# A post-norm decoder layer on one core: self attention by 32-row score strips with block turns on VectorE, and a new order around it

## What is computed

```python
# self attention: 16 heads of 64, no mask
q, k, v = split(x @ w_qkv)                     # (8, 16, 112, 64) each
attn = softmax(q @ k.T * 64 ** -0.5)
x = layernorm(x + (attn @ v) @ w_out + b_out)
# cross attention: 16 heads of 16, 375 keys, one mask for all
q, k, v = x @ Wq.T + bq, ctx @ Wk.T + bk, ctx @ Wv.T + bv
probs = softmax(where(mask == 0, -1e10, q @ k.T * 16 ** -0.5))
x = layernorm(x + (probs @ v) @ Wo.T + bo)
# one of 8 experts by argmax of x @ router.T, and a shared expert
y = down[e] @ (silu(gate[e] @ x) * (up[e] @ x))
x = layernorm(x + y + shared(x))
```

## Time and profile before

| | us |
|---|---|
| median of 3 runs | 432.59 (432.57 to 433.21) |
| profiled execution, its own time | 433.12 |
| its span, first to last instruction | 431.4 |
| TensorE busy | 408.3 (95%) |
| VectorE busy | 243.8 (57%) |
| ScalarE busy | 194.4 (45%) |
| GpSimd busy | 51.0 (12%) |

### The profile page before, as it was taken

The page is one execution under the profiler, slowest core; times in us unless marked ns, Lnnn a source line. Parts: engine busy times, 40 slices in busy tenths (PEclk is TensorE's granted clock), DMA queues, the critical chain, the costliest instruction groups (busy, mean ns, idle before and its releaser), DMA issues.

```text
span 431.4 us, 8970 instructions
## 1 busy us (share of the span) xinstructions
PE 408.3 (95%) x3130; PEld 287.5 (67%) x3131; DVE 243.8 (57%) x724; ACT 194.4 (45%) x580; POOL 51.0 (12%) x78
## 2 busy tenths in 40 slices
PE   8999999999999988999999999999988999999992
PEld 7767869778796855666666676666655475666661
DVE  1275765747566565666675767666764642244443
ACT  1164462433526446677567666766683101111220
POOL 4010010100101001000010101010100054212222
PEclk9999999999999999999999999999999999999998
DMA  8999000000000014040404050920000012112210
GB/s 249 364 378 274 12 0 2 0 2 2 1 2 0 2 37 147 2 183 2 185 2 183 7 179 4 366 108 2 2 2 2 1 62 98 57 56 68 70 40 28
DMA packets 15241, 34.25 MB, mean 79 GB/s; under 512 B 2381, under 2 KB 9150, under 8 KB 13920
## 3 DMA queue, kind: packets, MB, share of 16 engines
q1 hardware_dynamic: 13952, 30.72, 20.6%
q0 software_dynamic: 1104, 2.76, 1.8%
q10 hardware_dynamic: 144, 0.23, 0.2%
HBM read 27.27 MB, written 6.70 MB: 79 GB/s over the span
## 4 chain that ended last, share of the span: by engine, by line
PE 86%; DVE 5%; ACT 4%; issue 3%; POOL 0%; POOLq 0%; DVEq 0%; ACTq 0%
PE bank L437 11%; PE bank L638 9%; PE bank L451 7%; PE bank L619 6%; PE bank L507 6%; PE bank L815 6%; PE bank L536 5%; PE bank L655 4%; PE bank L905 4%; PE bank L881 4%; PE bank L887 4%; PE bank L529 4%; PE bank L468 3%; PE bank L494 3%; PE bank L827 3%
## 5 line engine op out<-in xcount | busy, mean ns | idle before, releaser
L1264 DVE CUSTOM_DVE_ANT_0 p<-bank,mask 112x375 f32<-112x375 f32 x128 | 62.7, 545 | 36.9 <-PE bank L619 36.9
L1023 ACT ACTIVATE p<-p,nm 112x375 f32<-112x375 f32 x128 | 74.4, 604 | 2.1 <-DVE nm L1264 2.0
L1030 ACT ACTIVATE pT<-bank 128x336 f32<-128x336 f32 x96 | 42.3, 441 | 44.4 <-PE bank L638 44.4
L638 PEld LDWEIGHTS bank<-ident,p 112*128 112x128 f32 (+1 forms) x384 | 38.1, 140 | 28.4 <-issue 23.1
L638 PE MATMUL bank<-ident,p 112*128 112x112 f32 (+1 forms) x384 | 53.8, 267 | 2.2 <-DVE nm L1264 2.0
L437 PE MATMUL bank<-x2T,arena 128*128 128x224 f32 x256 | 52.9, 354 | 0.0
L966 ACT ACTIVATE p<-bank,nm 112x112 f32<-112x112 f32 x128 | 43.5, 365 | 18.4 <-DVE nm L1134 18.3
L437 PEld LDWEIGHTS bank<-x2T,arena 128*128 128x128 f32 x256 | 46.8, 191 | 0.2
L352 POOL TENSOR_TENSOR rstd<-veps,minus_half 128x1 f32<-128x1 f32 x14 | 7.7, 549 | 289.8 <-DVE veps L1160 289.8
L1134 DVE TENSOR_REDUCE nm<-bank 112x4 f32<-112x448 f32 x32 | 19.2, 620 | 24.1 <-PE bank L468 24.1
L619 PE MATMUL bank<-kT,qz 32*112 32x375 f32 x256 | 28.8, 517 | 4.0 <-ACT x2T L992 2.5
(11 more groups left out here) (144 smaller groups left out, 595.1 us busy)
## 6 DMA issues: line engine op xcount, KB each, us to landing
arena<-in_ug SPq DMA_DIRECT2D x8, 1024.0 KB, 5.8
arena<-in_dn SPq DMA_DIRECT2D x8, 512.0 KB, 6.9
mid<-in_ctxT SPq DMA_DIRECT2D x8, 375.0 KB, 3.1
slots_s<-blank SPq DMA_DIRECT2D x14, 128.5 KB, 3.8
arena<-in_wqk SPq DMA_DIRECT2D x7, 256.0 KB, 5.6
slots_x<-blank SPq DMA_DIRECT2D x14, 128.0 KB, 6.7
p<-slots_s SPq DMA_DIRECT2D x9, 128.5 KB, 2.1
kT<-slots_x SPq DMA_DIRECT2D x9, 128.0 KB, 2.2
```

Source lines behind the costliest of these rows:

```text
L638: mm = pe.transpose(PE_T2[r][0:k1 - k0, t * S:(t + 1) * S], p2_rows[:, i % RING, k0:k1], ident[0:S, 0:S])
L1023: act.activation(p2[i % RING], p2[i % RING], ACT.Exp, bias=nm2[:, i % H:i % H + 1], scale=-1.0).then_inc(exp2, 1)
L1030: act.activation(pT2[:, i % RING], PE_T2[r][:, 0:KT * S].rearrange("p (k n) -> p k n", k=KT), ACT.Copy).then_inc(pt2_act, 1)
L1264: v.tensor_tensor_reduce(p2[i % RING], PE_S2[r][0:S, 0:S2], bias[:], 1.0, 3e38, ALU.add, ALU.min, accum_out=nm2[:, i % H:i % H + 1]).then_ ...
```

## The change

- *Scores.* The 112 query rows are cut into 4 blocks of 32 (`SQ`, `QB`); in odd batches the last has 16 rows. A score matmul now has 32 query columns, so eight run side by side: 2 row halves (head parity) x 4 column strips (four heads). A bank holds, for each of four heads on its strip of 32 partitions, 4 blocks of rows by 112 keys.
- *Softmax* works on all 128 partitions; its tiles are laid out by strip.
- *Turns.* TensorE's turns and VectorE's copies go; VectorE turns 32x32 blocks from `p1` to `pT1` in SBUF (`turn_blocks`). `p1` is padded to 128 columns, zeroed once by GpSimd.
- *Values.* `value1` sums over four blocks of 32 keys; eight matmuls side by side: 4 row strips (heads) x 2 column halves (parity), into four banks, one for each strip. The two `evac_o` each wait for both pairs.
- *Value projection.* `project_v1` writes the values by strip: 32 token columns x 4 strips x 256 columns. The weights' columns are reordered on the host (`by_strip`).
- *Order of a batch.* `out1` moves behind the second score group and into half of bank 7; the query scale's matmul goes to bank `PE_J1[0]`, and `project_v1(3, 0)` waits for the scale. Values stand before the last two projections of the batch.
- *Cross attention.* `project_k(0, b + 1)` moves ahead of the turns 2 and 3 of slot g = 0. The norm is split: the sum at the start of slot 0, moments at its end. `evac_x2` goes from ScalarE to the end of slot 1 on VectorE. In the last slots `out2(5)`, `turn_x2(5)`, the first router products and shared-expert products are reordered.

```diff
-        bank = [ctx.enter_context(nc.psum_tensor(f"bank{j}", [128, 512], F32)) for j in range(8)]
+        banks = ctx.enter_context(nc.psum_tensor("banks", [128, 8 * 512], F32))
+        bank = [banks[:, j * 512:(j + 1) * 512] for j in range(8)]
...
-        PE_S1, PE_J1, PE_T1, PE_U1, PE_W1 = bank[0:2], bank[2:4], bank[4], bank[5:7], bank[7]
+        PE_S1, PE_J1, PE_U1, PE_W1 = bank[0:2], bank[2:4], bank[4:8], bank[7][:, 256:512]
...
             def project_v1(b, c):
...
-                for k in range(KC):
-                    mm = pe.matmul(PE_J1[c][0:S, :], xT[:, b // 2, k, (b % 2) * S:(b % 2 + 1) * S], wv1[:, c, k, :],
-                                   start=(k == 0), stop=(k == KC - 1))
+                if (b, c) == (3, 0):
+                    pe.wait_ge(prep, 7)
+                for j in (2 * c, 2 * c + 1):
+                    m = block1(j, b % 2 == 0)
+                    at = (b % 2) * S + j * SQ
+                    for k in range(KC):
+                        for strip in range(STRIPS):
+                            mm = pe.matmul(PE_J1[c][SQ * strip:SQ * strip + m, (j % 2) * 256:(j % 2) * 256 + 256],
+                                           xT[:, b // 2, k, at:at + m], wv1[:, strip // 2, k, (strip % 2) * 256:(strip % 2) * 256 + 256],
+                                           start=(k == 0), stop=(k == KC - 1))
...
             def score1(pair, b):
...
+                for i in range(QB):
+                    m = block1(i, b % 2 == 0)
+                    at = (b % 2) * S + i * SQ
+                    for strip in range(STRIPS):
+                        for par in range(2):
+                            r = slice(64 * par, 64 * par + 64)
+                            mm = pe.matmul(PE_S1[par][SQ * strip:SQ * strip + m, i * 128:i * 128 + S],
+                                           qT[b // 2 % 2][r, 4 * pair + strip, at:at + m],
+                                           kT[b // 2 % 2][r, 4 * pair + strip, cols_b], start=True, stop=True)
...
             def value1(pair, b):
-                pe.wait_ge(pt1, b * 4 + (2 * pair + 2))
+                pe.wait_ge(turned1, b * 4 + (2 * pair + 2))
...
+                if b >= 2:
+                    pe.wait_ge(y1, b - 1)
+                for j in range(QB):
+                    n = block1(j, False)
+                    for par in range(2):
+                        at = (2 * pair + par) * D1
+                        for strip in range(STRIPS):
+                            rows_s = slice(SQ * strip, SQ * strip + n)
+                            mm = pe.matmul(PE_U1[strip][64 * par:64 * par + 64, pair * S:(pair + 1) * S],
+                                           v1[b % 2][rows_s, j, at:at + D1], pT1[2 * pair + par][rows_s, j, 0:S],
+                                           start=(j == 0), stop=(j == QB - 1))
...
             for b in range(B):
                 score1(0, b)
+                between1(b, 0)
+                between1(b, 1)
+                score1(1, b)
                 if b >= 2:
                     out1(b - 2)
...
                 between1(b, 2)
-                turn(1, b)
                 between1(b, 3)
-                turn(2, b)
+                if b < B - 1:
+                    value1(0, b)
+                if 2 <= b < B - 1:
+                    value1(1, b)
                 between1(b, 4)
-                turn(3, b)
                 between1(b, 5)
-                value1(0, b)
-                value1(1, b)
+                if b == B - 1:
+                    value1(0, b)
+                if b < 2 or b == B - 1:
+                    value1(1, b)
...
-                if (g, place) == (0, 2) and 1 <= b < B - 1:
+                if (g, place) == (0, 0) and 1 <= b < B - 1:
...
+            def turn_blocks(g, b):
+
+                v.wait_ge(norm1, b * 4 + (g + 1))
...
+                v.transpose(pT1[g].rearrange("p j (i a) -> p i j a", i=QB),
+                            p1[g].rearrange("p i (j a) -> p i j a", j=QB)).then_inc(turned1, 1)
...
                 if (g, place) == (0, 0) and b >= 3:
-                    ln2_a(b - 3)
+                    ln2_add(b - 3)
                 if (g, place) == (0, 3) and b >= 1:
                     evac_v(2, b, PE_L2)
+                if (g, place) == (0, 4) and b >= 3:
+                    ln2_a(b - 3)
+                if (g, place) == (1, 3) and b >= 3:
+                    evac_x2(b - 3)
```

More of the change, by code:

```diff
@@ L50 @@
 S_PAIR = 2 * S
+SQ = 32
+QB = -(-S // SQ)
 def build(nc, a, out):
@@ L442, in project_v1 @@
                 if b == 0:
-                    pe.wait_ge(w_v[c], 16)
+                    for half in range(2):
+                        pe.wait_ge(w_v[half], 16)
                     pe.wait_ge(qk_sb, 7 + c)
@@ L742, in between @@
                     project_v(1, b + 1, PE_L2)
-                if (g, place) == (3, 2) and b >= 2:
+                if (g, place) == (3, 2) and 2 <= b < B - 1:
                     out2(b - 2)
@@ L831, in _ @@
             pe.wait_ge(w_loaded["shared"], 32)
+            pe.wait_ge(max2, SLOTS * STRIPS)
+            shared(0, 0, range(0, 1))
             value2(SLOTS - 1)
-            logits_first()
+            shared(0, 0, range(1, 2))
+            turn_x2(NT - 2, bank[1])
             pe.wait_ge(y2, NT - 1)
             turn_o(B - 1)
-            shared(0, 0, range(0, 1))
+            shared(0, 1, range(0, 1))
             turn_on(B - 1)
-            shared(0, 0, range(1, 2))
+            shared(0, 1, range(1, 2))
+            logits_first()
             out2(NT - 1)
-            shared(0, 1)
             shared(1, 0)
@@ L1051, in between @@
                     evac_x1(6)
-                if (g, place) == (1, 1) and b >= 3:
-                    evac_x2(b - 3)
                 if (g, place) == (3, 0) and b >= 1:
```

203 lines of the change are left out of this document (94 added, 109 removed).

## The result

| | before | changed |
|---|---|---|
| median, us | 432.59 (5 runs, 432.40 to 433.21) | 426.74 (5 runs, 425.94 to 428.63) |
| profiled execution, its span, us | 433.12, 431.4 | 428.63, 426.9 |

The ratio is 0.986, its 95% interval 0.9843 to 0.9878: faster by 1.4%, where 3.0% was forecast (419.5, range 415.5 to 430). The direction and the range held; more than half of the gain is missing. The profiled execution is the slowest of its five, 1.9 above the median, so a part of what it shows the others did not have.

A forecast was written before the change was run, and what follows sets the result against it. TensorE, busy for 95% of the span, was taken to bound the kernel. Self attention -9.3 and the rest -3.8 gave -13.1 us: 433.12 to 420.0 profiled, 419.5 median; range 415.5 to 430, the forecast's own 416 to 423.

The forecast's parts named there:

- own sign: Self attention: the prediction called itself wrong if this did not end 8 to 11 us earlier.
- covered by its idle time: VectorE's block turns in self attention: 0.7 us each, 0.1 more four times a batch, hidden in VectorE's idle time.
- Values, 0 us: Value groups of self attention: 128 matmuls for 32, eight at once, still 16 steps of 0.097 us, so no added time.
- Batch 7, -0.5: Last self-attention batch: a new 2.9 us wait before the second scores, yet 17.0 for 17.6; range -2 to +1.
- rival 1: Scores and values: only four small matmuls run at once, +24.9 us, 444.4, slower; chance 0.12.
- the 446: Kernel time estimated from the skill's 25 ns issue gap, with a step of eight at 0.2 us.
- The steady batch: Self attention, batches 2 to 5: 18.55 less 1.56 for turns plus 0.19 for shapes, 17.2 us, -1.37 each.
- Batch 0: First self-attention batch: 16.2 us to 14.4, put at -1.7, or -1.6 with 0.1 for the second score group's wait.
- key projection: Cross attention, slot 0: moved before the turns, it fills TensorE's 0.43 us wait in batches 1 to 6, -2.6.
- the norm: Cross attention, norm and x2 copy: -0.1 three times in slot 1, +0.4 in batch 7, together +0.1 us.
- rival 3: New covers fail: second score groups +3.2, batch 7 +1.5, later norm in slot 1 +2.5 us; 426.7; chance 0.13.
- Rival 2: VectorE's block turn is slow, 1.3 us, delaying the values by about 1 us a batch; 427.5; chance 0.10.

The follow-up runs named there:

- eleventh run: Changed kernel with the first score group of batch 3 alone issued four times over; 432.38 us in its one run.
- fifth: Changed kernel with GpSimd's addition of the output bias held until VectorE's fourth block turn of the batch; 426.08 us, ratio 0.9838.
- sixth: Changed kernel with VectorE's fourth product and turn ahead of the norm's moments and first query/key evacuation in batches 2 to 6; 426.10 us, ratio 0.9840.
- third: Changed kernel with six matmuls of no use in TensorE's 3.03 us wait of batch 7; 425.09 us, ratio 0.9827.
- eighth: Changed kernel with VectorE's last norm step behind the second mask in slot 1 of cross attention, batches 3 to 7; 424.23 us, ratio 0.9810.
- tenth: Changed kernel with the loads for cross attention and shared expert, and the zeroing, spread to later points; 426.81 us, ratio 0.9858.
- fourth: Changed kernel with the loads from the output weights on held until the seventh query/key piece is done; 428.25 us, ratio 0.9889.
- the first experiment: Kernel before, with only the change's new order of cross attention and tail; 429.26 us, ratio 0.9921.
- 9: Changed kernel with batch 7 of self attention in a new order on TensorE and VectorE; 422.51 us, ratio 0.9751.

## Why the prediction was right and wrong

By its own sign the prediction was wrong: self attention had to end 8 to 11 us earlier and ended 1.4 earlier (162.16 to 160.76). The steps that failed, in its own terms: the fourth block turn, *covered by its idle time*, was not, because VectorE's product before it took 1.14 us beside GpSimd's addition and came late in VectorE's order (0.5 a batch); *Values, 0 us* measured +0.3 a batch; and *Batch 7, -0.5* measured +1.8, as the wait was put in without what it does to the clock and to the query evacuation.

- **Eight at once: right.** Score groups 1.01 and value groups 1.06; rival 1, four at once, is out, and so is the 446 beside it: in the eleventh run matmuls start 12.2 ns apart. By the starts, a step of eight takes 0.100 to 0.103 us in the score groups (0.106 in one) and 0.111 to 0.113 in the value groups, under the 0.148 at which the change loses.
- **The steady batch: its sum was off by 0.9**, in two halves. *Values, 0 us* was the first: 16 steps at 0.097 were taken (by the starts 0.099 before), they take 0.112, and values 2.0 for 1.69. With +0.07 for the scores, +0.06 for the value projection and +0.13 for the query/key pieces, less the 0.19 for shapes, this is 17.6. Why a step of values is longer than one of scores, when eight run in both, no run isolates; the supply of instructions, blamed in the eleventh expectation, let a score group run at 0.098. The second half was *covered by its idle time*: VectorE has the time on average, but its fourth product met GpSimd's addition and stood behind the norm's moments, where TensorE needed it next. 0.5 a batch, shown by the fifth and sixth runs.
- **The second score groups: right.** The cover holds; steady waits of about 0.1 were forecast and are there. Batch 1 waits 0.41.
- **Batch 7: the wait was right (3.03 for 2.9), its price wrong.** Forecast -0.5 with +1 as the worst, measured +1.8. Missing were the clock behind the wait (1.4 here, third and eighth runs) and a wait of 1.17 for the query evacuation, which the change puts behind the fourth turn. Where the clock stays up that wait is 1.44, and batch 7 is still 0.5 longer than before.
- **Batch 0: -1.6 forecast, 0.0 in this execution,** because of the stop of 1.37; executions without a stop have 14.3 to 14.8, next to the forecast's 14.4. 16.2 less 14.4 is 1.8, not the 1.7 of the prediction.
- **The start: 0 forecast, +1.3 measured, and by the traces it is the clock.** The first seven of the 64 query/key matmuls are 374 ns apart, the rest 189. A window over them prints a granted clock of 1.00, but the trace has no record of the clock there: its first, at full clock, begins at 7.4 us, just where the spacing changes, and in the trace of before at 5.1, where these matmuls start. The later the first record, the longer the 64 take, by about half the delay: 12.27 us with 5.0 (tenth), 12.42 with 5.4 (third), 12.70 with 6.0 (fourth), 13.42 with 7.4 (change). The kernel of before has 5.1 and 5.4 in its two profiles, the changed ones 4.5 to 7.6; whether the change has a part in that is not shown.
- **Cross attention: the key projection gives 0.65 a slot for 0.43** (slot 0 from 5.72 to 5.07), **the norm costs more**: +1.2 in slot 1 of batch 4, where +0.1 was put on all. The +0.4 of batch 7 came as forecast. The sum had the norm before the maxima, and left out that a query projection behind them waits for ScalarE's key copy. That was rival 3's third part, with another place. That the 3.8 of the forecast is also what the first experiment gives by the starts is luck: two wrong sizes cancel.
- **Tail: -0.9 for -1.3**, with a wait of 0.76 at the last x2 turn where 0.6 was put.
- **Rivals.** Rival 3 named 426.7 and the median is 426.74. That is luck: its parts were 3.2 for second score groups that wait no longer than forecast but for batch 1, 1.5 for batch 7 and 2.5 for the norm, and the measured loss lies in batches 3 to 5 (2.4 us), batch 7 (2.2), batch 0 (1.6) and the start (1.3). Rival 2 fell with the 0.71 of the turn. The time lies in the stated range only because the range had been widened for rivals 2 and 3; the forecast's own, 416 to 423, it misses.

The stop and the late clock differ from one execution to the next: the profile lost 8.6 us against the forecast, the median 7.2. Three parts of the loss are shown to come back by order alone (6, by its trace, 8 and 9). Put together they bring 417.5, near the low end of the forecast's range, but with a kernel that the forecast was not about.

## What to carry to other kernels

When full-width matmuls become many small ones on tiles, count what arrives as well as what runs: here eight at once started every 0.098 us, but some 256 instructions, a fetch, cover only 128 matmuls, and a fetch that a load in flight or too dense a stretch makes late stops TensorE. A long wait of TensorE is priced with the work behind it at half clock, and here was cheapest to mend by what VectorE does first, not by what TensorE is given. One trace is one execution: clock falls and stops for instructions differ from one to the next, so look at several before a difference is put down to the edit. And take a rate from starts, not from lengths with a tail in them. And where an engine has idle time on average, look for the one instruction that is needed next, and what runs beside it.

## What the hardware showed that was not expected

- A wait of 3.03 us of TensorE was followed by half clock in seven of eight profiles, at 1.0 to 2.6 us; six matmuls of no use in it kept the clock up (batch 7 17.99 for 19.35).
- A VectorE product with two SBUF inputs takes 1.14 us beside a GpSimd addition of 0.74, and 0.62 apart; a 128x256 norm step 0.82 for 0.37.
- TensorE stops of 0.3 to 2.3 us at the arrival of its instructions, at other lengths in each execution, as long as the fetch is late, with DMA engines full or, at 512 instructions in 3.2 us, idle.
- Eight tiles of 112 fp32 columns start every 0.098 us for long rows of scores, 12 ns a matmul.
- A VectorE turn of 32x32 blocks on 128x512 fp32 takes 0.71 us.
